# A norm's power moved on GpSimd, and a ring of PSUM banks cut from eight to six, in the attention of a four-stage kernel

## The reference, cut to what matters

```python
x = x + attn_a(layernorm(x))     # x: (4, 1024, 256)
x = x + ffn(layernorm(x), ...)
x = x + attn_b(layernorm(x), w_q, w_k, w_v, w_o)
x = x + ffn(layernorm(x), ...)

def layernorm(x):
    return (x - mean(x)) / sqrt(var(x) + 1e-5)

def attn_b(x, w_q, w_k, w_v, w_o):          # 16 heads of 64, causal
    q, k, v = einsum(x, w_q), einsum(x, w_k), einsum(x, w_v)
    a = softmax(where(causal, q @ k.T / 8, -inf))
    return (a @ v) @ w_o

def ffn(x, gate_w, w1, w2):                 # 8 experts, each takes its 256 best tokens of a sequence
    g, m = top_k(softmax(x @ gate_w.T).transpose, 256)
    return scatter_add(m, g * (gelu(x[m] @ w1) @ w2))
```

## Time and profile before

| | |
|---|---|
| median of 3 runs | 2149.88 us (2149.3 to 2153.25) |
| the profiled execution, its own time | 2147.21 us |
| its span | 2145.7 us |
| PE busy | 2057.5 us, 96% of the span |
| DVE, POOL, ACT busy | 1414.9, 1377.2, 904.7 us |
| granted PE clock, mean | 0.992 |

### The profile page before, as it was taken

The page is one execution under the profiler, slowest core; times in us unless marked ns, Lnnn a source line. Parts: engine busy times, 40 slices in busy tenths (PEclk is TensorE's granted clock), DMA queues, the critical chain, the costliest instruction groups (busy, mean ns, idle before and its releaser), DMA issues.

```text
span 2145.7 us, 35631 instructions
## 1 busy us (share of the span) xinstructions
PE 2057.5 (96%) x13666; PEld 1598.7 (75%) x13666; DVE 1414.9 (66%) x3095; ACT 904.7 (42%) x1303; POOL 1377.2 (64%) x1238
## 2 busy tenths in 40 slices
PE   7998999999999999999999999999899999999998
PEld 5445888889786776767667766667666688899997
DVE  7375698585648667456766567874967646975554
ACT  6202553354334544335444244442444335444443
POOL 4313676677538877647778367753867937777774
PEclk9999999999999999999999999999999999999999
DMA  4533554556330001011110111101100245545552
GB/s 138 188 102 104 151 125 100 137 142 164 78 99 30 21 28 43 11 40 61 40 50 11 40 40 60 40 21 40 45 16 2 65 157 143 122 118 126 138 147 31
DMA packets 133785, 172.31 MB, mean 80 GB/s; under 512 B 16872, under 2 KB 109040, under 8 KB 133616
## 3 DMA queue, kind: packets, MB, share of 16 engines
q1 hardware_dynamic: 109040, 136.47, 20.0%
q0 software_dynamic: 24576, 33.57, 9.5%
HBM read 130.03 MB, written 39.85 MB: 79 GB/s over the span
## 4 chain that ended last, share of the span: by engine, by line
PE 67%; DVE 12%; POOL 6%; issue 4%; ACT 2%; DMA 1%; SPq 1%; POOLq 0%; DVEq 0%; ACTq 0%
PE psum L1406 12%; PE psum L1427 11%; PE psum L1576 9%; PE psum L1554 9%; PE psum L1477 7%; PE psum L1607 5%; PE psum L1491 4%; POOL t_acc L2598 3%; PE psum L1515 2%; PE psum L1592 2%; DVE psum L2331 2%; DVE f_hlo L2299 1%; DVE f_hhi L2297 1%; DVE t_mx L2362 1%; DVE f_wlo L2270 1%
## 5 line engine op out<-in xcount | busy, mean ns | idle before, releaser
L2598 POOL TENSOR_TENSOR t_acc<-t_acc,t_p 128x1024 f32<-128x1024 f32 (+2 forms) x254 | 416.8, 1647 | 21.3 <-POOL t_acc L2598 0.4
L1870 ACT ACTIVATE t_p<-psum 128x1024 f32<-128x1024 f32 (+2 forms) x291 | 292.4, 1019 | 85.3 <-PE psum L1554 76.0
L2515 POOL TENSOR_TENSOR f_wlo<-f_wst,f_whi 128x256 fp32r<-128x256 f32 x256 | 222.4, 946 | 164.3 <-ACT f_whi L1798 164.3
L1427 PE MATMUL psum<-f_whi,f_hhi 128*128 128x256 f32 x992 | 286.2, 289 | 8.6 <-DVE f_hlo L2299 8.5
L1427 PE MATMUL psum<-f_whi,f_hlo 128*128 128x256 f32 x992 | 280.3, 283 | 0.0
L1427 PE MATMUL psum<-f_wlo,f_hhi 128*128 128x256 f32 x992 | 280.1, 282 | 0.0
L2297 DVE CAST f_hhi<-f_h 128x512 fp32r<-128x512 f32 x256 | 140.6, 549 | 211.2 <-ACT f_h L1818 210.6
L1818 ACT ACTIVATE f_h<-psum 128x512 f32<-128x512 f32 x256 | 153.4, 600 | 282.7 <-PE psum L1406 269.7
L1576 PE MATMUL psum<-t_p,t_v 128*64 128x512 f32 (+3 forms) x1536 | 258.8, 486 | 1.5 <-POOL t_p L2578 1.5
L2612 POOL TENSOR_TENSOR t_yT<-t_pvs,t_den 128x512 f32<-128x512 f32 x64 | 84.3, 1317 | 260.0 <-ACT t_pvs L1880 230.9
L1576 PEld LDWEIGHTS psum<-t_p,t_v 128*64 128x64 f32 x1536 | 108.3, 137 | 162.3 <-issue 148.0
(11 more groups left out here) (307 smaller groups left out, 4669.2 us busy)
## 6 DMA issues: line engine op xcount, KB each, us to landing
f_wst<-in_L_ffn_w SPq DMA_DIRECT2D x64, 1024.0 KB, 5.8
t_wk<-wkT SPq DMA_DIRECT2D x32, 256.0 KB, 3.6
t_wq<-wqT SPq DMA_DIRECT2D x32, 256.0 KB, 3.8
t_wv<-wvT SPq DMA_DIRECT2D x16, 512.0 KB, 3.7
normal<-f_xy SPq DMA_DIRECT2D x5, 1024.0 KB, 5.4
a_x<-in_L_attn_a_x SPq DMA_DIRECT2D x4, 1024.0 KB, 7.5
res<-a_x SPq DMA_DIRECT2D x32, 128.0 KB, 2.7
t_xy<-res SPq DMA_DIRECT2D x4, 1024.0 KB, 6.3
```

What stands on the lines that cost most here:

```text
L1427: m = pe.matmul(out, h[:, js], w[:, f, :], start=(f == 0 and a == 0 and j % 2 == 0), stop=(f == FT - 1 and a == 2), skip_group_check=True)
L1870: act.activation(t["group"][group], k.bank_pair[odd // 2][:, :, 0:k.group_width(group)], ACT.Exp, scale=1.0 / float(np.sqrt(k.DH))).then_i ...
L2515: m = pool.tensor_tensor(t["wlo"][n % 2][:, i, ks], t["wst"][:, i, ks], t["whi"][n % 2][:, i, ks].bitcast(F32), ALU.subtract)
L2598: pool.tensor_tensor(acc[:, :, q0:], (p0 if kt == 1 else acc)[:, :, q0:], p[:], ALU.add).then_inc(k.p_acc, 1)
```

## The change

`norm_scale` on POOL is now called `norm_power`, a step of its own. With `apart=True` (the six norms made in attention) there is a `yield` between DVE's scale and POOL's power, and the stream then stands still until `state["turn"]` is set. That happens at two places: in `row_halves`, just ahead of the scores of tile (1, 2), if the stream already stands there (`state["apart"]`), and in `prepare`, which pumps the stream empty. The three pumps left out before are gone. The ring of `units` has banks 6 and 7 only once, at its start, and then six turns of banks 2, 3, 0, 1, 4, 5.

```diff
 def norm(self, x, y, stats, mv, rstd, ready, apart=False):
         self.norm_scale(n, stats, mv, rstd)
+        if apart:
+            yield
+        self.norm_power(n, rstd)
         yield
 def paced(norm):
             for n, _ in enumerate(norm):
                 yield
-                if n == 4:
-                    yield from [None] * 3
+                while n == 4 and not state["turn"]:
+                    state["apart"] = True
+                    yield
+                state["apart"] = False
 def prepare(b):
             self.v_load(b, 0)
+            state["turn"] = True
             for _ in state["rows"]:
                 pass
+            state["turn"] = False
 def row_halves(u):
                 if what == "score":
+                    if (1, 2) in group and state["apart"] and u < U - 1:
+                        state["turn"] = True
+                        pump(state["rows"])
+                        state["turn"] = False
                     self.scores(u, group, pair)
 def units():
-            self.work_ring = [6, 7, 2, 3, 0, 1, 4, 5]
+            self.work_ring = [6, 7] + 6 * [2, 3, 0, 1, 4, 5]
 class GpSimd
-    def norm_scale(self, run, stats, mv, rstd):
+    def norm_power(self, run, rstd):
```

More of the change, by code:

```diff
@@ L483 @@
     constants = candidates = attention_constants = score_constants = stores_done = skip
-    norm_stats = norm_scale = norm_rows = skip
+    norm_stats = norm_scale = norm_power = norm_rows = skip
     gate_load = gate_transpose = skip
@@ L516, in run, with norm @@
         self.barrier()
-    def norm(self, x, y, stats, mv, rstd, ready):
+    def norm(self, x, y, stats, mv, rstd, ready, apart=False):
         n = self.runs
@@ L841, in attention @@
         early = t["early"]
-        state = dict(values=None, stored=0, rows=iter(()), normal=0, scored=0, last=False, ended=False)
+        state = dict(values=None, stored=0, rows=iter(()), normal=0, scored=0, last=False, ended=False, apart=False,
+                     turn=False)
         maxima = k.max_parts()
@@ L860, in between @@
                 yield from paced(self.norm(t["xy"], t["xy"], t["stats"], t["mv"], t["rstd"],
-                                           [(sem, DMA * b) for sem in k.q_xout]))
+                                           [(sem, DMA * b) for sem in k.q_xout], apart=True))
                 state["normal"] = b
@@ L872, in between @@
                 self.norm_of["t", b + 1] = self.runs
-                yield from paced(self.norm(t["xy"], t["xy"], t["stats"], t["mv"], t["rstd"], [(k.q_x, DMA * (2 + b))]))
+                yield from paced(self.norm(t["xy"], t["xy"], t["stats"], t["mv"], t["rstd"], [(k.q_x, DMA * (2 + b))], apart=True))
         def prepare(b):
             self.v_load(b, 0)
+            state["turn"] = True
             for _ in state["rows"]:
                 pass
+            state["turn"] = False
             for c in range(NC):
```

## The result

The changed kernel takes 2206.26 us (median of 4 runs, 2204.5 to 2209.51) against 2149.59 us for the kernel before (2149.24 to 2153.25): a ratio of 1.0261, 95% interval 1.0244 to 1.0279, so 56.7 us slower. The direction was as predicted; the time is 24 us above the prediction and 4 us above the top of its range. The profiled execution took 2207.63 us, its span is 2205.9 us (2145.7 before) and its mean granted clock 0.978 (0.992 before).

The account below looks back on a forecast made before the run. PE, busy 96% of the span, was taken to bound the kernel. Terms -6.1 + 17.6 + 2 + 13.1 + 2.4 + 3 gave +32 us on 2147.2, so 2179.2, or 2182 us as median; range 2164 to 2202.

Parts of the forecast that it names:

- gain of the early power: Units 9, 12, 17 and 25: scores no longer wait for DVE's totals behind the power, 1.53 us each, -6.1 us.
- drains before units 14 and 22: Power and norm rows issued at once by prepare ahead of the transposes: 8 + 1.6 + 8 = 17.6 us.
- rows amid POOL's sums: Units 1, 10, 18, 26: norm rows come while POOL still sums and hold DVE up; 0 to 6, 2 us taken.
- ring, the nine waits of units 6-8, 14-16, 22-24, with clock: First divide waits for bank 2's reader, 2.45, 0.75 or 0.55 us each, plus 2.4 us of clock: 13.6 us.
- ring, the start: First projections ahead of unit 0 with the new ring, priced by half of the row above: 0.4 us.
- ring, elsewhere: Divide's wait for a value product in unit 27 and a row_scores in units 10 and 18: 1.6 us.
- row of scores beside the late rows: Units 10 and 18: a row_scores taking bank 2, priced within the 1.2 us it shared with the first projections.
- route: Route's DVE work shifts by half a unit, some waits go and others grow; -4 to +8, 3 us taken.
- Some 5 to 8 us: Route wait of line 1345 of before, with DVE crowded ahead of it, instead of 1.2 us.
- The clock: Lower granted clock behind long PE pauses: 1.6 us at the drains and 2.4 at the 2.45 us ring waits.
- The cheap drain: Rival: in units 14 and 22 DVE gets in at every boundary, 9 instead of 17.6; +21.5, 2171 us; 22%.
- Strict exclusion: Rival: DVE instructions each wait for a POOL sum; drains 24, rows 6, route 8; +47, 2197 us; 18%.

Follow-up runs that it names:

- power_only: The changed kernel with the old ring of eight banks, powers and rows standing as in the changed kernel: 2178.28 us, 1.0117 of the kernel before.
- ring_only: The kernel before with the new ring of banks alone, powers where they were: 2174.77 us, 1.0107 of the kernel before.
- before_thin: The kernel before with most of POOL's second-half sums cut to 4 columns: 2136.06 us, 0.9919 of the kernel before.
- pause5: The kernel before with the pause ahead of DVE's shift five steps instead of three, power and ring untouched: 2148.41 us, 0.9991 of the kernel before.
- power_flag: The changed kernel with the old ring and the flag apart set one pump earlier, leaving no rows for prepare: 2162.49 us, 1.0047 of the kernel before.
- score_bank1: The changed kernel, but the row of scores takes bank 1 where it would get bank 2: 2191.64 us, 1.0189 of the kernel before.
- pause_pick: The kernel before with five pause steps for all attention norms except the one in the route, which keeps three: 2149.78 us, 0.9987 of the kernel before.
- thin sums: The changed kernel with most of POOL's second-half sums cut to 4 columns, the rest left out: 2155.16 us, one time taken.

## Why the prediction was too low

By its own terms, first as predicted, then as the pitches of power_only and ring_only show them (the start is read from the changed kernel):

| term | predicted | measured |
|---|---|---|
| gain of the early power | -6.1 | -6.1 (taken as four at 1.53; seen by itself in unit 12, -1.52) |
| drains before units 14 and 22 | +17.6 | +17.5 (10.6 and 6.9) |
| rows amid POOL's sums | +2 | +6.6 |
| ring, the nine waits of units 6-8, 14-16, 22-24, with clock | +13.6 | +13.2 |
| ring, the start | +0.4 | +2.0 |
| ring, elsewhere | +1.6 | +4.9 |
| row of scores beside the late rows | in the two above | +7.7 |
| route | +3 | +6.1 |
| units 29 to 31 | 0 | +4.2 |
| sum | +32 | +56.1 |

The changed kernel's own pitches give 57.5 us (55.5 and the 2.0 of the start), so 1.4 are in no row; the clock drop of 1.7 us in unit 6, which ring_only's profile doesn't have, is about that. The 7.7 is what units 9 to 11 and 17 to 19 have in the changed kernel above power_only, 9.2 us, less the 1.5 that ring_only loses there too, which stands a row higher.

*Placements.* The list of takes and pumps was right: the powers fell where it said, the divide waits in the named units with 2.42, 0.68 and 0.52 us against 2.45, 0.75 and 0.55 (the rows shown give 2.43, 0.70 and 0.52, nearer still), line 1566 waits for the totals once, for 0.2 us near the end, line 1357 waits once. "Some 5 to 8 us" was forecast for that last wait; it is 6.2.

*The gain.* Right in unit 12, and shown twice more without the change: in before_thin (1.53, 1.53 and 1.49), and in part in pause5. In units 9, 17 and 25 it is mixed with the rows or the route.

*The drains.* The sum was right to 0.1 us, in part by luck: unit 14 cost a microsecond more than forecast, unit 22 one less, and what they are made of is different. The forecast was 16 us of delay and 1.6 of clock; in power_only the 17.5 are 12.3 us of waits and 5.2 of longer busy time. (For unit 22 the prediction's text says 7.5 and its sum takes 8.) power_flag removes the drains and wins 15.8 us.

*The step that failed* is "Units 10 and 18, a row_scores, and the first projections ahead of unit 0: 1.2 in all, by half of the row above each", together with "Nothing on PE hangs on them until the totals" in the part on the rows. Each sentence was reasoned as if the other edit were not there. With the old rows the copy of the row of scores is in time (ring_only); with the old ring nobody wants its bank (power_only). With both, DVE's copy stands behind rows held up by the sums, and the divide waits 3.69 us, twice, plus lower clock. The interaction is 7.7 us more than the edits apart by the pitches (8 by the medians), the largest single part of the 24 us by which the sum was too low and enough to carry the time out of the range; and moving that one take to another bank gave back 12.5 by the pitches: all that those four units had cost above the kernel before. That is more than 7.7 because two clock drops of 1.7 us, which power_only has there, didn't come either.

*Rows amid the sums.* 2 was taken from a range of 0 to 6, and 6.6 came. Net of the 1.53 us that they gain, units 10 and 18 lose 1.2 and 1.7 us even with the old ring, where PE waits 1.36 us for ACT's e_yT, the transposed rows. Half of the 6.6 is clock: in unit 10 power_only has 0.95 where score_bank1, with the same rows and the same wait for e_yT, has 1.00. The stretch from the first divide of unit 10 to that of unit 11 in power_only, then in score_bank1:

```profile
992.51:1027.82 35.31, 35.31 (x262) 25.28 (x261) 23.41 (x53) 15.32 (x20) 25.44 (x25) 0.95 0.21 66
```

```profile
996.94:1030.58 33.64, 33.64 (x263) 24.79 (x262) 23.42 (x53) 15.31 (x20) 25.45 (x25) 1.00 0.22 69
```

*The clock.* It runs through most rows of the table and was priced too low. The prediction adds 4.0 us for it (1.6 and 2.4). From unit 0 to 31 PE's busy time, with the same instructions, grew by 10.1 us in power_only, 6.6 in ring_only and 18.7 in the kernel after.

*Ring.* The nine places worked out from rows were right together, 13.2 us, again by parts that cancel. The wait for the maxima cost 2.47 and 2.49 us in units 6 and 14 but 0.94 in unit 22, where the wait ahead of it for t_xTlo shrinks from 2.46 to 1.04 us; and the clock fell behind two of the three waits, 1.7 us each, where 0.8 had been put on each of three. The start, priced "by half of the row above", cost 2 us. The 4.9 elsewhere is ring_only's: it has value waits of 0.68 us in units 11, 19 and 20 and a longer unit 25. The changed kernel has the one of unit 27 in place of these, as predicted, so this row is the loosest of the table.

*Route and tail.* The route's 6.1 is inside its bounds of -4 to +8. The tail was not in the sum at all; pause_pick and power_flag show that it follows from how DVE and POOL fall together there and can come with either of these edits absent.

*The rivals.* The cheap drain is refuted by 10.6 us in unit 14. "Strict exclusion" was nearest in time (2197) and near the mechanism, but the nearness in time is luck: its 24 us for the drains were 6.5 too many, and its +47 lacked the interaction, the start and the tail. (The lower end of the range is meant to be the cheap drain less 5 us, which is 2166 and not 2164.)

*What stays open.* The 6.1 us of the route were not taken apart further; its waits (4.7 and 6.2 us) stand behind DVE work that both the rows and the sums delay, and thin sums reduce them to 1.6 and 3.9. Of ring_only, 2.2 us from unit 19 to 20 are 0.7 of a value wait and 1.5 of longer busy time at a granted clock of 0.95 (1.00 before), and 1.1 in unit 25 is longer busy time at 0.91 (0.96 before); why the clock fell there was not tested.

## What to carry to other kernels

When two edits are costed apart, ask once more at each place which both touch: here a late reader and a bank that comes round sooner were each harmless alone. A step moved "where nothing hangs on it" goes into a queue; price what stands behind it there, at the durations it has beside the other engine's work, not at its own. And a gain that comes from unblocking a queue may be had by moving the blocked instruction (five pumps of pause) instead of what it waits for; here it brought no more than 1 to 5 us in pause_pick, since the tail took most of it back.

## What the runs showed of the chip

- These instructions of DVE, from SBUF to SBUF, end with POOL's: a 128x8 shift 0.17 us alone, 2.30 beside a sum of 128x1024; four rows of 128x256 1.46 us alone, 5.61 beside them. In units 10 and 14 of the kernel after, one or two of DVE's short instructions were let in at each boundary between POOL's sums: the rows of unit 10 took 0.40, 0.98, 2.32 and 2.02 us. The other way a mask of 0.41 us took 3.10. DVE's t_neg, which reads PSUM and one tile of SBUF, took 1.2 us in all 32 units, beside POOL's sums too.
- The same pause does not always cost clock. Behind the 2.42 us wait of unit 6 the granted clock over the next 9 us was 0.81 in the kernel after and 1.00 in score_bank1, with the same instructions ahead; the unit differs by 1.7 us. Behind the same wait in units 14 and 22 of ring_only the next unit is 1.7 us longer by the clock, behind that in unit 6 it isn't. Stretches of the two, in that order:

```profile
842.70:851.70 9.00, 8.97 (x40) 3.33 (x42) 1.68 (x3) 0.59 (x1) 2.90 (x3) 0.81 0.01 2
```

```profile
843.20:852.20 9.00, 8.96 (x50) 3.54 (x52) 3.01 (x6) 0.59 (x1) 2.88 (x3) 1.00 0.01 2
```

A single profile can't tell such 1.7 us from an effect of an edit.
